# Cross-attention: projecting V for two steps at a time, with 256 moving columns, in seven groups of two key tiles

## What is computed

```python
B, N, D, M, DC = 8, 256, 128, 1601, 96      # sequences, tokens, channels, context keys, context channels
H, DH = 16, 64                               # heads, width of a head
def _attn(xq, ctx, wq, wkv, wo, bo):
    q = _heads(xq @ wq)
    k, v = jnp.split(ctx @ wkv, 2, axis=-1)
    k = _heads(k)
    v = _heads(v)
    q = _rope(q, sq, cq)
    k = _rope(k, sk, ck)
    sim = jnp.einsum('bhnd,bhmd->bhnm', q, k) * DH ** (-0.5)
    a = jax.nn.softmax(sim, axis=-1)
    o = jnp.einsum('bhnm,bhmd->bhnd', a, v)
    o = o.transpose(0, 2, 1, 3).reshape(xq.shape[0], xq.shape[1], MID)
    return o @ wo + bo
ctx_n = _ln(context, ca_lnc_w, ca_lnc_b)
x = _attn(cross_in, ctx_n, ca_wq, ca_wkv, ca_wo, ca_bo) + x
```

## Time and profile before

| | |
|---|---|
| median of 3 runs | 1980.28 us (1977.44 to 1980.57) |
| the profiled execution | 1978.65 us, its span 1976.9 us |
| busy share of the span | TensorE 97%, VectorE 79%, GpSimd 64%, ScalarE 50% |
| mean granted TensorE clock | 0.994 of full speed |

### The profile page before, as it was taken

One profiled execution on the slowest core, in us unless ns is written; L12 is line 12 of the kernel. 1 busy time (PEld: TensorE's weight loads), 2 busy tenths in 40 slices (PEclk: granted clock), 3 DMA queues, 4 the chain that ended last, 5 costly groups with the idle time before them and its releaser, 6 DMA issues.

```text
span 1976.9 us, 54053 instructions
## 1 busy us (share of the span) xinstructions
PE 1918.3 (97%) x20976; PEld 1345.7 (68%) x20976; DVE 1557.0 (79%) x2292; ACT 982.1 (50%) x1588; POOL 1263.5 (64%) x814
## 2 busy tenths in 40 slices
PE   6989999988999999999999999999999999999999
PEld 4667776755666776767767766666766667666674
DVE  4888888876887888888888888878888888878851
ACT  3555555544445544544554544455454445545455
POOL 4777765423766766676767667667666767676662
PEclk9999999998999999999999999999999999999999
DMA  5322223211111111111111111111111111111110
GB/s 178 101 81 80 76 87 98 76 41 48 51 55 52 55 60 50 50 50 56 52 56 58 50 50 51 56 51 56 58 50 50 52 55 51 58 56 49 47 34 22
DMA packets 110872, 118.92 MB, mean 60 GB/s; under 512 B 26528, under 2 KB 74784, under 8 KB 110624
## 3 DMA queue, kind: packets, MB, share of 16 engines
q1 hardware_dynamic: 110624, 115.46, 17.6%
HBM read 36.71 MB, written 1.05 MB: 19 GB/s over the span
## 4 chain that ended last, share of the span: by engine, by line
PE 81%; POOL 5%; DVE 4%; DMA 4%; issue 3%; SPq 1%; ACT 1%; DVEq 0%; POOLq 0%; ACTq 0%
PE S L1387 19%; PE OB L1401 17%; PE PB L1326 9%; PE PB L1339 8%; PE S L1358 7%; POOL psum_acc L702 3%; PE OB L1256 2%; DMA qswapped<-qturned 2%; PE PB L1410 2%; PE S L1228 2%; DMA swapped<-turned 2%; PE PB L1311 2%; PE PB L1184 1%; PE PB L1420 1%; PE PB L1213 1%
## 5 line engine op out<-in xcount | busy, mean ns | idle before, releaser
L702 POOL TENSOR_TENSOR psum_acc<-psum_acc,P 124x1024 f32<-124x1024 f32 (+1 forms) x320 | 689.7, 2155 | 111.3 <-ACT P L845 93.9
L845 ACT ACTIVATE P<-S 124x1024 f32<-124x1024 f32 (+1 forms) x448 | 431.3, 963 | 467.9 <-PE S L1387 466.1
L1062 DVE TENSOR_REDUCE mxc<-S 128x2 f32<-128x1024 f32 x384 | 469.0, 1221 | 89.0 <-PE S L1358 88.4
L1401 PE MATMUL OB<-P,V 124*64 124x256 f32 (+1 forms) x3328 | 428.5, 381 | 0.0
L695 POOL TENSOR_TENSOR psum_acc<-P 124x1024 f32<-124x1024 f32 x64 | 152.3, 2380 | 321.4 <-ACT P L845 321.4
L1401 PEld LDWEIGHTS OB<-P,V 124*64 124x64 f32 (+1 forms) x3328 | 223.8, 136 | 132.3 <-issue 40.6
L1387 PE MATMUL S<-QH,KH 64*124 64x256 f32 (+1 forms) x1664 | 254.8, 302 | 1.3 <-ACT P L845 1.3
L1027 DVE TENSOR_TENSOR turned<-PB,rope 128x512 f32<-128x512 f32 (+1 forms) x256 | 146.1, 571 | 120.4 <-PE PB L1326 120.0
L722 ACT ACTIVATE V<-PB 124x512 f32<-124x512 f32 (+1 forms) x320 | 156.6, 489 | 169.2 <-PE PB L1339 82.9
L1387 PE MATMUL S<-QL,KH 64*124 64x256 f32 (+1 forms) x1664 | 234.8, 278 | 0.0
L1387 PE MATMUL S<-QH,KL 64*124 64x256 f32 (+1 forms) x1664 | 234.8, 278 | 0.0
(11 more groups left out here) (163 smaller groups left out, 3001.3 us busy)
## 6 DMA issues: line engine op xcount, KB each, us to landing
swapped<-turned SPq DMA_DIRECT2D x512, 128.0 KB, 2.1
kv_w<-sa_kv_dram SPq DMA_DIRECT2D x64, 128.0 KB, 2.3
qswapped<-qturned SPq DMA_DIRECT2D x128, 64.0 KB, 1.9
kv_w<-ca_kv_dram SPq DMA_DIRECT2D x64, 96.0 KB, 2.2
ctxT_all<-ctx_dram SPq DMA_DIRECT2D x8, 624.0 KB, 4.6
q_w<-sa_wq_dram SPq DMA_DIRECT2D x64, 64.0 KB, 2.0
q_w<-ca_wq_dram SPq DMA_DIRECT2D x64, 64.0 KB, 1.9
o_w<-ca_wo_dram SPq DMA_DIRECT2D x64, 64.0 KB, 2.0
```

Of the source, the lines that this page charges most:

```text
L702: pool.tensor_tensor(acc, acc, P_of(J, c)[0:rows, :, 0:w], ALU.add).then_inc(x.acc, 1)
L845: act.activation(P_of(J, c)[0:rows, :, 0:w], SP[0:rows, :, 0:w], ACT.Exp, scale=SCALE).then_inc(x.e, 1)
L1062: dve.tensor_reduce(mxc[:, t, :, c:c + 1], MP[:, :, 0:w], AX.X, ALU.max).then_inc(x.am, 1)
L1401: ins = pe.matmul(OB[half(h), 0:N], Vb[J % 2][0:w, t, half(h)], P_of(J, c)[0:w, h, k * N:(k + 1) * N], start=(t == 0), stop=(t == len(a_.t ...
```

## The change

V is projected for steps J and J+1 (J even) in one go. The moving operand of each product is then the V weights of both steps, 2 x 128 = 256 columns, taken from two neighbouring weight buffers, which are now slices of one tensor. A group is two tiles instead of four, so that it still fills the bank `XB`; there are seven groups (six of two tiles and one of one tile) for two steps. The table `V_WORDS` gives the groups to the words v0 to v3: an even step's words do groups 0, 1, 2 and 6, an odd step's words v0 to v2 do groups 3, 4 and 5, and its v3 does nothing. The word `v3+-1` stands in the next body, so group 6 is done in the body of the odd step. ScalarE copies each group into both V buffers with one instruction, whose output has the two steps as an inner dimension. `v_count` counts groups in the order in which they are done, and the waits for V and for the weight buffers are put in its terms.

```diff
-        self.vgroups = [list(range(a, min(a + 4, len(self.tiles)))) for a in range(0, len(self.tiles), 4)]
+        self.vgroups = [list(range(a, min(a + 2, len(self.tiles)))) for a in range(0, len(self.tiles), 2)]
...
-        kv_w = [sb(f"kv_w{i}", [D, 2 * PAIR]) for i in range(UNROLL)]
+        kv_ws = sb("kv_w", [D, UNROLL, 2 * PAIR])
+        kv_w = [kv_ws[:, i, :] for i in range(UNROLL)]
...
-        Vb = [sb(f"V{i}", [D, len(CROSS.tiles), PAIR]) for i in range(2)]
+        Vbs = sb("V", [D, 2, len(CROSS.tiles), PAIR])
+        Vb = [Vbs[:, i, :, :] for i in range(2)]
...
+        V_WORDS = ((0, 1, 2, 6), (3, 4, 5, None))
+
+        def v_group(J, k):
+
+            return V_WORDS[J % 2][k]
+
+        def v_count(J, g):
+
+            done = [v for words in V_WORDS for v in words if v is not None]
+            return J // 2 * NV + done.index(g) + 1
...
             def cross_weights(J, pair):
-                wait(sp, x.vp, times(J, NV) - (UNROLL - 1) * NV)
+                wait(sp, x.vp, (J - UNROLL) // 2 * NV + NV)
...
-                def read_v(J, g):
+                def read_v(J, k):
+                    g = v_group(J, k)
+                    if g is None:
+                        return
+                    J -= J % 2
                     ts = a_.vgroups[g]
                     w = a_.tiles[ts[0]][1]
-                    wait(act, x.vp, times(J, NV) + g + 1)
-                    wait(act, x.pv, times(J, NU) - 2 * NU + min((ts[-1]) // 2, NU - 1) + 1)
-                    copy(Vb[J % 2][0:w, ts[0]:ts[-1] + 1, :],
-                         XB[0:w, 0:len(ts) * PAIR].rearrange("p (t n) -> p t n", n=PAIR)).then_inc(x.ve, 1)
+                    wait(act, x.vp, v_count(J, g))
+                    wait(act, x.pv, times(J - 1, NU) + g + 1)
+                    copy(Vbs[0:w, :, ts[0]:ts[-1] + 1, :].rearrange("p i t n -> p t i n"),
+                         XB[0:w, 0:len(ts) * 2 * PAIR].rearrange("p (t i n) -> p t i n", i=2, n=PAIR)
+                         ).then_inc(x.ve, 1)
...
-                readers = {"q": (x.qc, lambda K, k: K + 1), "v": (x.ve, lambda K, k: K * NV + k + 1),
+                readers = {"q": (x.qc, lambda K, k: K + 1), "v": (x.ve, lambda K, k: v_count(K, v_group(K, k)) if v_group(K, k) is not None else None),
...
-                def project_v(J, g):
+                def project_v(J, k):
+                    g = v_group(J, k)
+                    if g is None:
+                        return
+                    x_free(uses, readers, J, ("v", k))
+                    J -= J % 2
                     loaded(J)
+                    loaded(J + 1)
                     if J == 0:
                         wait(pe, z.added, B)
-                    x_free(uses, readers, J, ("v", g))
                     for k, t in enumerate(a_.vgroups[g]):
                         lo, w = a_.tiles[t]
                         lo += batch(J) * M
                         for a, b in ((0, DH), (DH, w)):
-                            ins = pe.matmul(XB[a:b, k * PAIR:(k + 1) * PAIR], ctxT_all[0:DC, lo + a:lo + b],
-                                            kv_w[J % UNROLL][0:DC, PAIR:2 * PAIR], start=True, stop=True)
+                            ins = pe.matmul(XB[a:b, k * 2 * PAIR:(k + 1) * 2 * PAIR], ctxT_all[0:DC, lo + a:lo + b],
+                                            kv_ws[0:DC, J % UNROLL:J % UNROLL + 2, PAIR:2 * PAIR],
+                                            start=True, stop=True)
                     ins.then_inc(x.vp, 1)
...
-                    wait(pe, x.ve, times(J, NV) + a_.units[c][-1] // 4 + 1)
+                    wait(pe, x.ve, v_count(J, c))
```

## The result

The median after the change is 1989.64 us (1985.23 to 1994.37, 8 runs) against 1980.44 us (1977.44 to 1983.2, 8 runs) before. The ratio is 1.0045 (95% interval 1.0031 to 1.0058). So the kernel became 9 us slower, where I had forecast 2 us less and had ended my range at 1984.0. The profiled execution took 1990.83 us with a span of 1989.0, 12.1 us more than the span of before.

A forecast was written before the change was run, and what follows sets the result against it. TensorE's own work bounds the kernel (busy 1918.3 of 1976.9 us). The profiled 1978.65 us less 2 us, other costs nothing, is 1976.65; as a median 1978.3, stated as 1978.2 us. Range for 8 in 10: 1973.5 to 1984.0 us.

The forecast's parts named there:

- TensorE's own work: V projection: 1664 pair passes of 128 columns become 832 of 256, saving 2 us, with ends 0 and 4.2 us.
- Costs at nothing: Side effects of the change on weights, copies, buffers, products and waits: all covered by slack, put at 0 us.
- weights: Weight loads lie under the matmul before; SyncE's even-step loads go some 2 us later, 5 us to spare; no cost.
- copies: ScalarE's copies of V stay at 597 ns; they may become 2.5 times as long before TensorE waits.
- buffers: ScalarE's new wait before writing a V buffer is over when the projection is done; no cost.
- products: Even step's units 3, 4, 5 need v0, v1, v2 of the following body; 3.2, 2.4, 1.5 us to spare.
- the extra wait: TensorE's wait for the second step's weights: costed at nothing; 224 at 20 ns, 4.5 us, kept for the range.
- Rival D: Today's TensorE waits change with the bodies' phase, by at most 3.2 us; faster, about 1974.5 us; chance 0.04.
- A: Real fixed cost per pass of the V projection; faster by over 0.2%, mostly 1970 to 1976 us; chance 0.14.
- B: V projection's moving operand in two pieces costs TensorE 832 times; slower, 1986.5 us at 10 ns a break; chance 0.08.
- C: Late copy for v2 delays even step's unit 5 of products (1.5 us slack); 4 us needs 0.19 each; chance 0.04.

The follow-up runs named there:

- e8: Kernel after, with the last tile projected for each step alone, 128 columns in every body, other six groups still paired; 1978.7 us, ratio 0.9981.
- e3: Kernel before, with one wait changed so that even steps load K, V and q weights only after v2 of the body before; 1983.26 us, ratio 1.0001.
- e12: Kernel after, with 15 (even steps) or 6 (odd) idle wait words from step 15, making bodies of 512 TensorE instructions; 1987.58 us, ratio 1.0023.
- e5: Kernel after, with each V product of 256 columns made as two of 128 again; 1990.46 us, ratio 1.004.
- e16: e13 with the 15 idle words of an even step spread, two or three behind each of six scores' words; 1989.65 us, ratio 1.0043.
- e14: e8 with 6 idle wait words a body (24 in the first nine), making bodies of 512 TensorE instructions; 1977.61 us, ratio 0.9972.
- e15: e8 with 16 idle wait words in the first five bodies, then 6, so blocks fall elsewhere than in e14; 1982.01 us, ratio 1.0.
- e13: Kernel after with the idle words of e12, begun six steps earlier (step 9); 1986.5 us, ratio 1.0025.
- e9: Kernel before, with the last tile of both steps projected in the odd body and none in the even one; 1983.73 us, ratio 1.001.

## Why the prediction was wrong

**TensorE's own work: right.** I forecast 0.06 us less for two bodies, 0.91 us for a group behind scores, the means of the products for the new matmuls, and waits on ScalarE in no body. The rows show 45.89 for 45.94 us, 0.91 us, 387 ns (the products have 381), and 0.2 us of waits on ScalarE, once. The gain was there: 1.3 to 1.6 us in the bodies where I took 2. That e8, which keeps it and adds no stalls, ran at 1978.7 us where the text says 1978.2 is luck: before stood at 1983.27 beside it.

**Costs at nothing: the step that failed.** The part weighed weights, copies, buffers, products and the extra wait, each by its own slack, and each held: e3 shows the late weights free, and the one wait for V (0.2 us in body 11) came from a late swap. The 20 ns for a wait on the path had no row behind it; e12 now shows 23 ns for each of ten in a row, and the range had room for it. What the part left out, and so put at nothing, is the instructions themselves as traffic, and with it the slack of the swaps. TensorE's stream is carried by the DMA rings in blocks of 16 KB. With the change, a block came late over the swap of K's second chunk in 13 bodies, where before it did in none, and these bodies stalled by 8.9 us. The page of before had the line for it (174 packets of kind "instruction"), and I did not ask where they fall. That they moved because there are 3328 instructions fewer is only argued. e5 has the old matmuls in the new order of groups, with 174 packets as before, and is as slow: 4 late packets over K's swap cost it 3.6 us, and those over Q's 7.9.

**Rival D: right in kind, capped wrongly.** It said that the waits of today change with the phase of the bodies, "by at most the 3.2 us that they sum to", and counted only on the side of faster. Nothing caps a wait by its present sum. The swap has little slack: VectorE needs it 3.04 us after its issue, a packet at 0.3 to 0.9 us is mostly covered, and one at 1.6 us or later is not. The waits became 11.8 us. Nothing of D went into the upper end of the range, 1984.0, because of this cap.

**Rivals A, B and C: rightly put low.** A fixed cost of a pass (A) of 5 ns or more would show as bodies shorter by 0.13 us for two, and they are 0.05 shorter. A break in the moving operand (B) would make a group longer than 0.91 us, and e5, without the break, is no faster. Late V (C) shows no wait of the products. The single wait for V's copy, in body 11, is that of the next projection for the bank, not of unit 5.

**What stays open.** That a late fetch makes the swap late and stalls the body is shown by the twin bodies of e16, and that moving blocks moves the time by e14 against e15. Not settled is what sets the moment of a fetch. In e16 it alternates between bodies with the same place in their blocks, with a period of four bodies, which is 2048 instructions or eight packets; and e12 and e13 missed the place that I had worked out from the kernel after. So I can't say why its even bodies drew the late fetches and its odd ones none. About as many packets fall over Q's swap in e5 as before (17 and 16), and they cost more (6.2 against 1.9 us of waits on GpSimd's sums). Here the moment of the packet goes far to explain it: one under 1.0 us after the issue costs little (0.8 us for 11 of them before), one at 1.2 to 2.4 us costs more (2.7 us for 7 before), and e5 has 11 of the later kind, which stall it by 6.5 us. Each of them still costs e5 half as much again as before, and why is not shown.

## What to carry to other kernels

When TensorE is 99% busy and its waits are a few us, the slack of the transfers behind it decides whether a small saving arrives: list each round trip over DMA, its landing time and what covers it, and ask what 1 to 2 us more would cost in every body. A long unrolled program is traffic of its own; look at the queue of kind "instruction" on the page and at where its packets fall before and after a change in the number of instructions. e8 keeps what the pairing gives (1.6 us), leaves the bodies alike, and was the first version faster than both kernels (0.9981), and with its blocks moved off the swaps (e14) the ratio is 0.9972. That alike bodies are what helps is not shown: e9 has uneven ones and few stalls, and e15 is alike and no faster than before.

## What the runs showed of the hardware

TensorE's instructions come in packets of 16 KB on their own queue, 256 instructions each (3328 fewer took away 13 packets). In the kernel after, one of them some 1.7 us behind the issue of a pair of swaps of 128 KB goes with 4.2 to 4.9 us from the issue to the use of these, where it is 3.04 us without, and with 3.8 us for a load of 64 KB in place of 2.2.

Ten idle instructions, each with two waits for a count long reached, cost TensorE 0.23 us where they stand in a row between two groups, and nothing that shows where two or three stand together (most odd bodies of e16: 23.16 us).

A product on 124 columns of the array, between products on 64, is dearer than the pair of 64 and 60 that it replaces: 1.06 for 0.92 us a group of four tiles, and with the passes around it 0.94 us a body in all.
